# Value wave between the two score pairs, another layout for later one-hots, and column-tiled router products

## The reference

```
x = x + tanh(g_xattn) * attention(layernorm(x), ctx, ctx)   # 8 heads of width 4, softmax over 1601 keys
x = x + tanh(g_ffn)   * moe(layernorm(x))

attention: q = queries @ Wq + bq;  k = keys @ Wk + bk;  v = values @ Wv + bv    # width 32 = 8 x 4
           softmax(q k^T / sqrt(32)) v, heads joined, @ Wo + bo                  # back to 256
moe:       scores = softmax(x @ router_w + router_b)                             # 8 experts
           G, idx = top_k(scores.T, 512)                  # each expert picks 512 of the 2048 tokens
           y[idx] += (relu(x[idx] @ w1 + b1) @ w2 + b2) * G                      # 256 -> 1024 -> 256
```

## Time and profile before

| | us |
|---|---|
| median of three runs | 607.13 (607.10 to 607.14) |
| the profiled execution | 606.36 |
| its span, first to last instruction | 604.5 |
| TensorE busy | 561.3 (93%) |
| VectorE busy | 435.9 (72%) |
| ScalarE busy | 396.4 (66%) |
| GpSimd busy | 196.0 (32%) |
| mean granted TensorE clock | 0.995 |

### The profile page before, as it was taken

The page is one execution under the profiler, slowest core; times in us unless marked ns, Lnnn a source line. Parts: engine busy times, 40 slices in busy tenths (PEclk is TensorE's granted clock), DMA queues, the critical chain, the costliest instruction groups (busy, mean ns, idle before and its releaser), DMA issues.

```text
span 604.5 us, 12817 instructions
## 1 busy us (share of the span) xinstructions
PE 561.3 (93%) x5052; PEld 327.4 (54%) x5052; DVE 435.9 (72%) x797; ACT 396.4 (66%) x771; POOL 196.0 (32%) x192
## 2 busy tenths in 40 slices
PE   7799899989999989999999988899999999999994
PEld 3433333333343333443334344469889898898974
DVE  3889789996889967989895257745766767667541
ACT  2587799977989878888888820044654646646551
POOL 3058030043600244200185010230735527346234
PEclk9999999999999999999999999999999999999998
DMA  8600000000000000000000140012635547355133
GB/s 277 235 1 1 1 2 2 2 1 37 2 36 2 2 36 1 37 1 1 37 36 2 37 154 22 16 55 61 177 102 114 141 113 163 102 113 155 21 36 35
DMA packets 23807, 35.80 MB, mean 59 GB/s; under 512 B 3459, under 2 KB 16196, under 8 KB 23620
## 3 DMA queue, kind: packets, MB, share of 16 engines
q1 hardware_dynamic: 17604, 26.59, 13.2%
q0 software_dynamic: 6144, 8.39, 8.1%
HBM read 26.59 MB, written 8.39 MB: 58 GB/s over the span
## 4 chain that ended last, share of the span: by engine, by line
PE 66%; DVE 18%; ACT 5%; issue 4%; POOL 4%; DMA 1%; POOLq 0%; ACTq 0%; DVEq 0%; SPq 0%
PE ps L1616 15%; PE ps L1623 15%; DVE mquart L986 11%; PE ps L1408 11%; PE ps L1395 6%; PE ps L1374 5%; ACT probs L725 3%; PE ps L1304 2%; PE ps L1265 2%; POOL xn L513 2%; PE ps L1280 1%; PE ps L1452 1%; PE ps L1585 1%; PE ps L1594 1%; PE ps L1569 1%
## 5 line engine op out<-in xcount | busy, mean ns | idle before, releaser
L986 DVE TENSOR_REDUCE mquart<-ps 128x2 f32<-128x802 f32 x256 | 241.8, 987 | 35.2 <-PE ps L1374 32.0
L725 ACT ACTIVATE probs<-ps 128x512 f32<-128x512 f32 (+1 forms) x416 | 222.7, 599 | 24.1 <-PE ps L1395 21.1
L1408 PE MATMUL ps<-probs,vp 128*32 128x256 f32 (+1 forms) x1664 | 132.7, 391 | 4.4 <-ACT osb L625 4.4
L1374 PE MATMUL ps<-kpad,qrows 64*128 64x401 bf16 x512 | 90.2, 337 | 3.7 <-DVE mquart L986 3.1
L1233 DVE TENSOR_TENSOR h1l<-hf,h1h 128x512 fp32r<-128x512 f32 x64 | 44.3, 693 | 66.4 <-ACT hf L838 56.5
L1395 PE MATMUL ps<-qfull,kpad 64*128 64x256 bf16 (+1 forms) x832 | 89.2, 272 | 2.8 <-ACT x L746 0.9
L837 ACT ACTIVATE h1h<-ps,b1T 128x512 fp32r<-128x512 f32 x64 | 44.0, 687 | 58.0 <-PE ps L1616 57.8
L1623 PE MATMUL ps<-w2h,h1h 128*128 128x256 f32 x256 | 73.8, 288 | 2.1 <-DVE h1l L1233 1.5
L1623 PE MATMUL ps<-w2l,h1h 128*128 128x256 f32 x256 | 72.4, 283 | 0.0
L1623 PE MATMUL ps<-w2h,h1l 128*128 128x256 f32 x256 | 72.3, 282 | 0.0
L1395 PEld LDWEIGHTS ps<-qfull,kpad 64*128 64x128 bf16 (+1 forms) x832 | 38.7, 96 | 47.5 <-ACT probs L725 25.3
(11 more groups left out here) (175 smaller groups left out, 681.0 us busy)
## 6 DMA issues: line engine op xcount, KB each, us to landing
w1raw<-in_L_ffn_w SPq DMA_DIRECT2D x16, 512.0 KB, 4.9
w2raw<-in_L_ffn_w SPq DMA_DIRECT2D x16, 512.0 KB
xs<-in_x SPq DMA_DIRECT2D x4, 512.0 KB, 7.8
ctx_sb<-in_ctx SPq DMA_DIRECT2D x3, 512.0 KB, 5.9
out<-xs SPq DMA_DIRECT2D x3, 512.0 KB, 2.6
x_rows<-x SPq DMA_DIRECT2D x3, 512.0 KB, 2.6
b2b<-in_L_ffn_b SPq DMA_DIRECT2D x1, 1024.0 KB, 11.1
out<-xs SPq DMA_DIRECT2D x2, 256.0 KB, 2.0
```

The source lines that it names most:

```text
L725: nc.scalar.activation(out_p, ps[0:w, next_bank(), :], ACT.Exp, scale=float(SCALE)).then_inc(s_ex, 1)
L986: nc.vector.tensor_reduce(mquart[:, u % 2, t, a, :, kq], ps[:, b:b + 2, 0:MAXW], AX.X, ALU.max).then_inc(s_mr, 1)
L1374: last = mm(ps[:, bank + b, 0:MAXW], qrows[band(b), g, q:q + P], kpad[band(b), g, a, lo:lo + MAXW], start=True, stop=True)
L1408: last = mm(ps[32 * hh:32 * hh + 32, PV, 0:UW], vp[0:w, kt, g, hh, :], probs[0:w, step % PROBS, hh, :], start=(kt == 0), stop=(kt == NKT - 1))
```

## The change

Three parts. On each key tile the value wave is issued between pair 0 and pair 1 of the scores. For experts 2 to 7 the one-hot is laid out with the token's row innermost, so that the stationary operand of one tile is contiguous; the compared position is then repeated along the innermost axis. For chunks 0 to 2 the router weights, padded to 32 columns, are the stationary operand, x2T moves, the four tiles of a chunk go to four groups of 32 output partitions at once, and the result is taken out, transposed (`turn_router`) and taken again; the last chunk keeps the old form.

```diff
+FIRST_SLOTS = 2
+        rw_pad = ar("rw_pad", [P, KD, 32])
+        lgT = ar("lgT", [P, P])
+        by_tile = onehot[:, :, :].rearrange("p r t -> p (r t)").rearrange("p (t r) -> p t r", r=P)
...
                 pool.wait_ge(s_rwts, 80)
-                pool.wait_ge(s_lgr, 2 * (c + 1))
+                pool.wait_ge(s_lgr, c + 1)
...
             rstd_1(1)
+            nc.gpsimd.memset(rw_pad[:, :, :], 0.0).then_inc(s_rp, 1)
+            pool.wait_ge(s_rwts, 80)
+            pool.wait_ge(s_rp, 1)
+            nc.gpsimd.tensor_copy(rw_pad[:, :, 0:E], rw_sb[:, :, :]).then_inc(s_rp, 1)
             pool.wait_ge(s_bob, 1)
             add_bo(0)
...
-            def take_L(c, half, bank):
+            def take_R(c, bank):
-                act.wait_ge(s_R, 2 * c + half + 1)
-                t = CT * c + UQ * half
-                take(lg[:, t:t + UQ, :], ps[:, bank, 0:UQ * E].rearrange("p (t e) -> p t e", e=E), s_lgr)
+                act.wait_ge(s_R, c + 1)
+                take(lgT[:, :], ps[:, bank, 0:P], s_lt)
+            def take_L(c, bank):
+                act.wait_ge(s_R2, c + 1)
+                take(lg[:, CT * c:CT * c + CT, :], ps[:, bank, 0:P].rearrange("p (t j) -> p t j", j=32)[:, :, 0:E], s_lgr)
...
-                    if c > 0 and (r, kt) in ROUTER_AT:
-                        take_L(c - 1, ROUTER_AT.index((r, kt)), next_bank())
+                    if c > 0 and (r, kt) == ROUTER_AT[0]:
+                        take_R(c - 1, next_bank())
+                    if c > 0 and (r, kt) == ROUTER_AT[1]:
+                        take_L(c - 1, next_bank())
...
-                nc.vector.tensor_tensor(onehot[:, :, a:a + NT], iota_x[:, :, a:a + NT],
-                                        pos_row[:, n:n + NT].unsqueeze(1).to_broadcast([P, P, NT]), ALU.is_equal).then_inc(s_oh, 1)
+                if e < FIRST_SLOTS:
+                    out, row = onehot[:, :, a:a + NT], iota_x[:, :, a:a + NT]
+                    pos = pos_row[:, n:n + NT].unsqueeze(1).to_broadcast([P, P, NT])
+                else:
+                    out, row = by_tile[:, a:a + NT, :], iota_b[:, :].unsqueeze(1).to_broadcast([P, NT, P])
+                    pos = pos_row[:, n:n + NT].unsqueeze(2).to_broadcast([P, NT, P])
+                nc.vector.tensor_tensor(out, row, pos, ALU.is_equal).then_inc(s_oh, 1)
...
+            def router(c, bank):
+                pe.wait_ge(s_rp, 2)
+                pe.wait_ge(s_Xt, KD * (c + 1))
                 for k in range(KD):
+                    for t in range(CT):
+                        last = mm(ps[32 * t:32 * t + 32, bank, 0:P], rw_pad[:, k, :], x2T[:, k, P * t:P * t + P],
+                                  start=(k == 0), stop=(k == KD - 1))
+                last.then_inc(s_R, 1)
+            def turn_router(c, bank):
+                pe.wait_ge(s_lt, c + 1)
+                nc.tensor.transpose(ps[:, bank, 0:P], lgT[:, :], ident).then_inc(s_R2, 1)
...
                     scores(u, kt, 0)
-                    scores(u, kt, 1)
-                    for n in range(tiles_by(u, 2 * kt), tiles_by(u, 2 * kt + 1)):
-                        max_tile(n)
                     if kt > 1:
                         pv(u, kt - 2)
                     elif u > 0:
                         pv(u - 1, NKT - 2 + kt)
+                    scores(u, kt, 1)
+                    for n in range(tiles_by(u, 2 * kt), tiles_by(u, 2 * kt + 1)):
+                        max_tile(n)
...
-                    if c > 0 and (r, kt) in ROUTER_AT:
-                        half = ROUTER_AT.index((r, kt))
-                        router(c - 1, half, next_act((s_lgr, 2 * (c - 1) + half + 1)))
+                    if c > 0 and (r, kt) == ROUTER_AT[0]:
+                        router(c - 1, next_act((s_lt, c)))
+                    if c > 0 and (r, kt) == ROUTER_AT[1]:
+                        turn_router(c - 1, next_act((s_lgr, c)))
...
-                    last = mm(ps[:, 0, 0:5 * NT], onehot[:, :, t], dat_hit[:, t, :, :].rearrange("p s j -> p (s j)"),
+                    last = mm(ps[:, 0, 0:5 * NT], onehot[:, :, t] if e < FIRST_SLOTS else by_tile[:, t, :], dat_hit[:, t, :, :].rearrange("p s j -> p (s j)"),
```

More of the change, by code:

```diff
@@ L1448, in transpose_x2_half, with router_half @@
                 last.then_inc(s_X, 1)
[L1450 removed]
+            def router(c, bank):
+                pe.wait_ge(s_rp, 2)
+                pe.wait_ge(s_Xt, KD * (c + 1))
                 for k in range(KD):
[L1452 to L1459 removed]
+                    for t in range(CT):
[5 more added lines that the diff above has]
+                nc.tensor.transpose(ps[:, bank, 0:P], lgT[:, :], ident).then_inc(s_R2, 1)
+            def router_half(half, bank):
+                pe.wait_ge(s_Xt, KD * LAST + half + 1)
+                for i, t in enumerate(part_tiles(LAST, half)):
+                    for k in range(KD):
+                        last = mm(ps[:, bank, E * i:E * i + E], x2T[:, k, P * t:P * t + P], rw_sb[:, k, :], start=(k == 0), stop=(k == KD - 1))
                 last.then_inc(s_R, 1)
@@ L1561, in _ @@
             keep_busy(3)
-            router(LAST, 1, 2)
+            router_half(1, 2)
             keep_busy(13)
```

12 lines of the change are left out of this document (3 added, 9 removed).

## The result

The changed kernel takes 617.18 us (median of four runs, 615.32 to 620.83) against 607.13. The ratio is 1.0173, 95% interval [1.0124, 1.0222]. The forecast of slower was right and its size was not: 4.7 us were forecast and 10.1 measured, so 617.18 lies 5.4 us above 611.8 and 0.2 us outside the range.

A forecast was written before the change was run, and what follows sets the result against it. The prediction took TensorE alone to bound the third unit and TensorE and VectorE the last. Terms 12.5 + 5.4 - 6.8 - 2.9 - 3.5 = +4.7 us on the median of 607.13 gave 611.8 us, range 604 to 617.

The forecast's parts named there:

- three boundaries: Unit boundaries into units 4, 8 and 12, taken as covered by VectorE and so costing nothing.
- the job steps of unit 0: Three key tiles with side jobs in unit 0, taken as covered because VectorE paces that unit.
- Plain steps: Attention key tiles where no side job follows: the new order costs nothing, 1.07 us again.
- the second rival: Score bands do not overlap across a max tile: about 12 us more in steps without a job, 624 us; chance 0.10.
- the 41 steps at 0.33: Key tiles with side jobs, 52 less 11 taken as covered, each costing 0.33 us for a lone score pair: 13.5 us.
- Unit boundary: First wave of a unit waits longer for ScalarE to take the old result: 12 boundaries by 0.45, +5.4 us.
- Lone pairs: Score pairs standing alone beside side jobs in the attention: 13.5 less 1.0 for idle time, +12.5 us.
- waits that go: Pair 1's waits behind query projections, splitting copies, output projection and in the last two units disappear: -6.8 us, between 0 and 10.
- Router, -2.9: Two router jobs per chunk fall from 1.84 to 0.86 us together, in chunks 0 to 2: -2.9 us.
- One-hots and slots: Slot filling for six experts loads contiguous one-hots faster, 0.58 us each: -3.5 us; slower one-hot building on VectorE costs nothing.
- The first rival: Lone pairs fall into TensorE's waiting time, halving the lone-pair and boundary terms: 602.8 us, or about 605; chance 0.25.
- The slots' rival: Slots load no faster with the new one-hot layout: 615.3 us; chance 0.10.

The follow-up runs named there:

- the short reduction: VectorE's reduction cut to half of each max tile's columns: changed kernel 607.26 us; the one with new router, new one-hots and old attention order 590.86 us.
- router and slots: Changed kernel with the old order of the attention, keeping the new router and the new one-hot layout: 601.49 us, 0.9909 of the kernel before.
- slots_alone: Kernel before with only the new layout of the one-hots of experts 2 to 7: 602.98 us, ratio 0.994.
- the jobs behind the wave: Changed kernel with all side jobs issued directly behind the value wave, ahead of pair 1 and its max tiles: 611.03 us, ratio 1.0071.

## Why the prediction was right in sign and 5.4 us too low

Three steps of the prediction failed: what the placing on r = 1 waits for had no term, three boundaries and the job steps of unit 0 were taken as covered, and nothing was set for a clock that falls in half the runs. The router gave less than forecast besides. The order was forecast at 12.5 + 5.4 - 6.8 = 11.1 us and measured at 14.7 between the waves.

**Plain steps, nothing.** Right for 1.07: the bands overlap across a max tile, and the second rival fell. "Each band of rows gets the same columns as before" counted columns and not the banks, so it did not see that a second max tile waits for VectorE in other steps now. In a quiet unit that adds 0.97 - 0.69 = 0.28 us to the growth; over all units it is no loss, as the short reduction shows.

**The placing on r = 1, which had no term of its own.** The forecast counted it among the 41 steps at 0.33. It grew by 1.39 (1.39 to 2.78). Of this 0.60 stays with the short reduction (1.99), the lone pair and the second max tile; 0.79 goes, and 0.78 is what the subtraction lasts longer since the new timing puts it inside an operation of GpSimd. Three chunks make 2.3 us of that, the largest single piece of the 3.6 that the order is off. The forecast looked at GpSimd's queue only for the padding of the router's weights. No kernel moved that operation alone; the evidence is the timing, and the two kernels in which the subtraction starts elsewhere, takes 0.20 us and leaves the step at 1.98 and 1.99.

**Unit boundary, +5.4.** A mis-sized term, about 0.7 us too small. The 0.61 became 0.58, and taking off 0.17 for the max tile was right: 0.41 net for the 0.45 taken. Wrong was to leave out three boundaries as covered by VectorE. All those into units 1 to 14 grew by 0.58 or 0.59, the last by 0.49, which makes 8.6, less 15 x 0.17 for the tiles 6.1. A full VectorE earlier in a unit does not shorten a wait for ScalarE at its end.

**Lone pairs, +12.5, and waits that go, -6.8.** The price was right, 0.33 by the earlier trace rows against 0.32. On r = 1 the steps behind the two projections and the one with the splitting copy lose 0.48, 0.66 and 0.42 (1.83 to 1.35, 2.00 to 1.34, 1.49 to 1.07); less one max tile that moved on, 0.17, this is 1.39 for the forecast's 2 x 0.61 + 0.33 = 1.55. Together the two terms make 14.7 - 6.1 - 2.3 = 6.3 us for 5.7. That they come so near is in part luck, since the cover stood elsewhere than forecast. The steps of unit 0, taken as covered, were not: the unit grew by 1.30 from router and slots to the changed kernel, 0.57 of it the boundary. The steps on (2, 4) and (2, 12), counted at 0.33, grew by 0.12 (1.94 to 2.06) and fell by 0.05 (1.70 to 1.65). On (2, 4) the old order had waited for VectorE already, for the step is 1.66 there with the short reduction.

**Router, -2.9.** The jobs are 0.57 and 0.26 us as forecast (0.60 and 0.26). The first step gives back all of it (2.24 to 1.97), the second 0.52 of 0.73 (2.22 to 1.70). That is 0.79 per unit and 2.4 between the waves; the medians show 1.95, and the profiled run 1.8 by span, with its first wave 0.2 us later.

**One-hots and slots, -3.5.** Right. The filling takes 0.56 for 1.17 us in experts 2 to 7, 0.61 x 6 = 3.7, and 1.35 in the first two, where it waits for VectorE as before (1.33 and 1.35); the 1.17 named for these two was a misreading. The whole kernel shows 3.7. By starts the loads now come at (0.56 - 0.17) / 15 = 26 ns for 64. The Trainium skill's "TensorE: Matmul & The Clock Gate", section "Weight-path perf modes — Fast Weight Load (FWL) and DoubleRow", has the fast load work for strided weights as well; here the same 16 products with the same hits follow each other 2.5 times as fast when only the layout changes (`slots_alone` fills in 0.56 us too), so for a stride of 16 elements the measurement decides against it. The one-hots take 684 ns for 421, as forecast, and cost nothing: VectorE waits 55.9 us in total ahead of the subtraction for ScalarE, 56.5 before.

**The sum.** Parts -5.2 for -6.4 (by the runs, 601.49 - 606.64), order +14.7 for +11.1. By span the order is 13.7, mostly because the first wave of the changed kernel happens to start 0.8 us earlier. The median lies 1.9 above the fastest run, since two of the four runs have the lower clock (0.985 and 0.988), for which the forecast had nothing: 611.8 + 1.2 + 3.6 - 1.0 + 1.9 = 617.5 for 617.18. Without those two runs the time would have lain inside the range, with the order mis-sized all the same. The first rival, half of the split hidden, fell: the two steps with transposes in the third unit grew by 0.49 and 0.32, not by less than 0.2. The slots' rival fell too.

## What to carry to other kernels

When an instruction moves, list for each step which users of shared buffers it now holds, and who gives the buffers back; counting columns does not see that. List also the short operations that a step waits for, and what the other engines will be doing when these start: here a shift of 0.4 us turned one of 0.20 us into 0.97. A wait at a fixed place, such as the taking at a boundary, is paid at every such place: an engine that is full elsewhere in the unit is no cover for it. A wait that an order avoids is not gained until the next two steps are shown to be no longer; here it came back in one of them.

## What the runs showed of the hardware

- Products on different halves of the rows start out of program order. In the plain step above the program has pair 1, max tile, pair 0. The single starts are 276.445 (pair 1), 276.451 (max tile, rows 0 to 63), 276.565 (pair 1), 276.631 (pair 0), 276.674 (max tile, rows 64 to 127), 276.740 (pair 0). The trace names the line and not the rows; I assigned those by the program's order within a half. The Trainium skill's "TensorE: Matmul & The Clock Gate", Part 3, has matmuls start and end strictly in program order; across halves this trace shows otherwise, since a product of the max tile, written third, starts second; within a half nothing in it speaks against the rule.
- The granted clock can stay at 1.2 GHz for most of a unit in which TensorE is nearly always busy: 13.31 of 14.00 us busy at 0.52. The unit takes 20.13 us for 14.79. It was at 2.4 GHz in the unit before, which had the usual short waits.
- A small subtraction on VectorE (128 x 8, two inputs) that starts inside GpSimd's two-input operation on 128 x 512 (L386) lasts until 0.05 us behind its end: 0.97 us on r = 1 of three chunks, 0.20 where it starts 0.15 us ahead of that operation. With the jobs behind the wave it starts later inside it and takes 0.47. All 27 such cases in the nine traces that have them end 0.05 us behind GpSimd. Beside GpSimd's one-input operations of 1.22 us (L522, L532) it took 0.29 and 0.44 at most. Why is not shown.
- A reduction on VectorE that reads half the columns takes 575 ns for 985, and old and new order gained 9.9 and 12.9 us of span by it. The old order's quiet unit, with VectorE busy for 15.2 of 15.4 us and TensorE for 15.1, became only 0.26 us shorter (15.38 to 15.12): both were full and TensorE set it. Of the 9.4 us between the waves unit 0 gave 2.9 and unit 13 1.8.
